# Row maxima turned in 32x32 blocks on VectorE, and other turns put in pairs at six places of four groups

## What is computed

```python
def ffn(x):                      # on (4, 128) tokens in the reference's set-up, here on each sequence
    x = x + msa(layernorm(x, ln1_w, ln1_b), w_qkv, w_proj)      # 16 heads of 8
    return x + moe(layernorm(x, ln2_w, ln2_b), ...)             # 8 experts, hidden 512, best one by gate

x = x + 0.5 * ffn(_layernorm(x))
x = x + attn(_layernorm(x))      # 16 heads of 8, 4 key/value heads, rotary positions
x = x + 0.5 * ffn(_layernorm(x))
# each attention: scores = q @ k.T * scale; softmax over 512 keys; @ v
```

## Time and profile before

| | |
|---|---|
| median of 3 runs | 1510.23 us |
| lowest, highest | 1509.4, 1512.35 us |
| the profiled execution's own time | 1509.52 us |
| its span, first to last instruction | 1507.8 us |
| mean granted TensorE clock | 0.977 |
| TensorE matmul, VectorE, ScalarE, GpSimd busy | 1377.5, 1176.0, 1102.9, 646.7 us |

### The profile page before, as it was taken

One profiled execution on the slowest core, in us unless ns is written; L12 is line 12 of the kernel. 1 busy time (PEld: TensorE's weight loads), 2 busy tenths in 40 slices (PEclk: granted clock), 3 DMA queues, 4 the chain that ended last, 5 costly groups with the idle time before them and its releaser, 6 DMA issues.

```text
span 1507.8 us, 34954 instructions
## 1 busy us (share of the span) xinstructions
PE 1377.5 (91%) x12036; PEld 670.6 (44%) x12036; DVE 1176.0 (78%) x1898; ACT 1102.9 (73%) x2124; POOL 646.7 (43%) x983
## 2 busy tenths in 40 slices
PE   3899999999999997999999999999999999999995
PEld 1333333433338883333333333333333344335995
DVE  6888889888855348888888888888888888894541
ACT  2488877787785563888888888787878777777553
POOL 5224245542226683544364353323334543313753
PEclk8799999999999997999999999999999999999998
DMA  3644433433102425432333243333333333211234
GB/s 90 164 137 117 111 102 98 114 93 86 45 25 60 119 75 160 114 83 69 97 97 83 71 110 86 100 91 79 89 93 84 81 88 100 63 37 37 75 106 120
DMA packets 101485, 137.57 MB, mean 91 GB/s; under 512 B 29792, under 2 KB 72160, under 8 KB 101312
## 3 DMA queue, kind: packets, MB, share of 16 engines
q1 hardware_dynamic: 70768, 85.69, 19.9%
q0 software_dynamic: 24256, 45.31, 12.3%
q10 hardware_dynamic: 6288, 4.34, 1.0%
HBM read 79.05 MB, written 53.51 MB: 88 GB/s over the span
## 4 chain that ended last, share of the span: by engine, by line
PE 58%; DVE 28%; issue 7%; DMA 3%; POOL 2%; ACT 1%; SPq 0%; DVEq 0%; POOLq 0%; ACTq 0%
DVE maxima L1251 25%; PE banks L884 16%; PE banks L871 12%; PE banks L855 11%; PE banks L1610 4%; PE banks L912 4%; PE banks L1619 4%; PE banks L894 2%; PE banks L938 2%; PE banks L919 1%; DMA by_token<-work 1%; PE banks L954 1%; DVE split L1259 1%; DVE stats L1329 1%; DMA work<-sorted_x 1%
## 5 line engine op out<-in xcount | busy, mean ns | idle before, releaser
L1251 DVE TENSOR_REDUCE maxima<-banks 128x2 f32<-128x1024 f32 x768 | 924.1, 1222 | 154.9 <-PE banks L855 146.8
L1222 ACT ACTIVATE work<-banks 128x512 f32<-128x512 f32 x1536 | 829.6, 598 | 155.5 <-PE banks L871 140.6
L855 PE MATMUL banks<-K,Q 64*128 64x512 f32 x1536 | 568.2, 459 | 46.5 <-DVE maxima L1251 36.4
L871 PE MATMUL banks<-Q,K 64*128 64x512 f32 x1536 | 566.2, 450 | 0.5
L884 PE MATMUL banks<-work,V 128*18 128x256 f32 x6144 | 481.6, 386 | 1.5 <-ACT work L1222 0.8
L855 PEld LDWEIGHTS banks<-K,Q 64*128 64x128 f32 x1536 | 228.2, 189 | 200.8 <-DVE maxima L1251 135.4
L871 PEld LDWEIGHTS banks<-Q,K 64*128 64x128 f32 x1536 | 228.9, 185 | 177.4 <-ACT work L1222 128.3
L884 PEld LDWEIGHTS banks<-work,V 128*18 128x18 f32 x6144 | 103.3, 96 | 275.1 <-issue 199.8
L723 POOL TENSOR_TENSOR lo<-full,hi 128x512 fp32r<-128x512 f32 x40 | 51.1, 1278 | 245.6 <-ACT hi L1097 144.1
L1619 PE MATMUL banks<-w,work 128*128 x736 | 99.6, 279 | 0.6 <-ACT work L1653 0.6
L1673 DVE COPY work<-w 128x512 f32 x88 | 43.9, 499 | 71.8 <-PE banks L1610 58.6
(11 more groups left out here) (193 smaller groups left out, 1268.4 us busy)
## 6 DMA issues: line engine op xcount, KB each, us to landing
Q<-q_scratch SPq DMA_DIRECT2D x188, 128.0 KB, 2.6
K<-k_scratch SPq DMA_DIRECT2D x376, 64.0 KB, 2.5
Q<-zero_rows SPq DMA_DIRECT2D x182, 64.0 KB, 2.2
q_scratch<-hi POOLq DMA_DIRECT2D x40, 256.0 KB, 4.7
q_scratch<-lo POOLq DMA_DIRECT2D x40, 256.0 KB, 6.8
k_scratch<-hi POOLq DMA_DIRECT2D x20, 256.0 KB, 4.5
k_scratch<-lo POOLq DMA_DIRECT2D x20, 256.0 KB, 6.3
work<-sorted_x SPq DMA_DIRECT2D x76, 66.0 KB, 2.0
```

The lines of the kernel that those rows point to most:

```text
L855: fill(nc.tensor.matmul(bank, q4[parts(j), n % SLOTS, j // 2, qt * P:(qt + 1) * P], k4[parts(j), n % SLOTS, j // 2, :], start=True, stop=T ...
L871: nc.tensor.matmul(scp[x % EXPS][:, :], k4[parts(j), n % SLOTS, j // 2, kt * P:(kt + 1) * P], q4[parts(j), n % SLOTS, j // 2, :], start=Tr ...
L1222: nc.scalar.activation(prob[:, kt, j ^ 1, :], scp[x % EXPS][:, :], ACT.Exp, scale=SCALE).then_inc(s.probs, 1)
L1251: nc.vector.tensor_reduce(c.maxima[:, at:at + 9:8], c.banks[:, k * S:(k + 2) * S].rearrange("p (m n) -> p m n", m=2), AX.X, ALU.max).then_ ...
```

## The change

There are two parts. First, the row maxima no longer go through TensorE and PSUM. VectorE turns the split maxima, 128 x 32 in SBUF, in four blocks of 32x32, right behind the split. Each block then holds 32 of the 128 queries, so SP moves a group's rows with eight DMAs of 16 pieces of 128 B in place of two DMAs of 16 pieces of 512 B. The turn `rows` leaves the plan, and with it its share of the ring.

Second, the other turns of a batch are placed anew within four groups. Before, an FFN batch had turns after eight steps: (0, 0) rows, z; (0, 2) out, q; (1, 0) rows, n; (1, 2) gate; (2, 0) rows, k; (2, 2) out, v; (3, 0) rows, a; (3, 2) proj, where the first number is n mod 4. Now there are six: (0, 0) z; (0, 2) out, q; (1, 0) n, k; (1, 2) gate, v; (2, 2) out, a; (3, 0) proj. For an attention batch they are z; out, q; qs, k at (1, 0); ks, v at (2, 0); out, a; proj.

```diff
-CONSUMER = {"max": "dve", "rows": "dve", "out": "dve", "gate": "dve", "z": "act", "q": "act", "qs": "act", "k": "act",
+CONSUMER = {"max": "dve", "out": "dve", "gate": "dve", "z": "act", "q": "act", "qs": "act", "k": "act",
...
+        merged = 0 <= n < self.last
+        if merged and kt == 2 and self.attended(n + 1) is not None and n + 1 < self.last:
+            names += [("a", self.attended(n + 1))]
+        if self.attended(n) is not None and not merged:
             names += [("a" if kt == 0 else "proj", self.attended(n))]
+        elif self.attended(n) is not None and kt == 0:
+            names += [("proj", self.attended(n))]
...
         if r == 1 and self.has((n + 7) // G) and not self.ffn((n + 7) // G):
-            names += [("qs" if kt == 0 else "k", (n + 7) // G)]
-        if r == 2 and self.has((n + 6) // G):
+            names += [("qs", (n + 7) // G)] * (kt == 0) + [("k", (n + 7) // G)] * (kt == 2 * (not merged))
+        if r == 1 and merged and self.has((n + 7) // G) and self.ffn((n + 7) // G):
+            names += [("v" if kt else "k", (n + 7) // G)]
+        if r == 2 and merged and self.has((n + 6) // G) and not self.ffn((n + 6) // G) and kt == 0:
+            names += [("ks", (n + 6) // G), ("v", (n + 6) // G)]
+        if r == 2 and not merged and self.has((n + 6) // G):
...
-        if kt == 0 and 1 <= n + 1 < self.last:
-            names += [("rows", n + 1)]
...
             def rows_of_max(n):
                 g = n % SLOTS
-                if n:
-                    released(sp, "rows", n)
-                else:
-                    sp.wait_ge(s.first, 2)
+                sp.wait_ge(s.max_turned, n + 1)
                 for tile in range(2):
                     r = TILE * tile + ROWS
-                    sp.dma_start(c.Q[r:r + 2, ...].rearrange("i (a n) -> i a n", n=P),
-                                 c.maxT[16 * tile:16 * tile + 16, n % 2 * P:(n % 2 + 1) * P].bitcast(F32))
+                    dst = c.Q[r:r + 2, ...].rearrange("i (a b q) -> i a b q", b=4, q=32)
+                    for b in range(4):
+                        at = 32 * b + 16 * tile
+                        sp.dma_start(dst[:, :, b, :], c.maxT[at:at + 16, 32 * (n % 2):32 * (n % 2) + 32])
...
             def split_max(n):
...
+                if n >= 2:
+                    dve.wait_ge(s.max_rows[(n - 2) % SLOTS], 128 * ((n - 2) // SLOTS + 1))
+                dve.wait_ge(s.split, n + 1)
+                nc.vector.transpose(cols(c.maxT, 32 * (n % 2), 32), cols(c.split, 32 * (n % 2), 32).bitcast(F32))\
+                    .then_inc(s.max_turned, 1)
-            def turn_max(n):
...
-            def copy_rows(n):
...
-        c.maxT = sb("maxT", [32, 2 * P], F32R)
+        c.maxT = sb("maxT", [P, 2 * 32])
```

More of the change, by code:

```diff
@@ L359, in slot @@
             names += [("rank", self.ranked(n))]
-        if self.attended(n) is not None:
+        merged = 0 <= n < self.last
+        if merged and kt == 2 and self.attended(n + 1) is not None and n + 1 < self.last:
+            names += [("a", self.attended(n + 1))]
+        if self.attended(n) is not None and not merged:
             names += [("a" if kt == 0 else "proj", self.attended(n))]
+        elif self.attended(n) is not None and kt == 0:
+            names += [("proj", self.attended(n))]
         if self.renormed(n) is not None:
@@ L396, in stream @@
     if True:
-        s = sems(ctx, nc, f"s{label}", "filled freed evacuated first max_hi split recip max_rows:5 q_loaded:5 k_loaded:5 "
+        s = sems(ctx, nc, f"s{label}", "filled freed evacuated max_hi split max_turned recip max_rows:5 q_loaded:5 k_loaded:5 "
                  "scores probs pv out_copied links dve_links first_stored:2 var_ready std_ready normed renormed stats:2 moments:2 added combined roped hi lo:2 "
@@ L594, in rows_of_max @@
                 g = n % SLOTS
-                if n:
-                    released(sp, "rows", n)
-                else:
-                    sp.wait_ge(s.first, 2)
+                sp.wait_ge(s.max_turned, n + 1)
                 for tile in range(2):
                     r = TILE * tile + ROWS
-                    sp.dma_start(c.Q[r:r + 2, g * KSLOT:(g + 1) * KSLOT].bitcast(F32).rearrange("i (a n) -> i a n", n=P),
-                                 c.maxT[16 * tile:16 * tile + 16, n % 2 * P:(n % 2 + 1) * P].bitcast(F32))\
-                        .then_inc(s.max_rows[g], 16)
+                    dst = c.Q[r:r + 2, g * KSLOT:(g + 1) * KSLOT].bitcast(F32).rearrange("i (a b q) -> i a b q", b=4, q=32)
+                    for b in range(4):
+                        at = 32 * b + 16 * tile
+                        sp.dma_start(dst[:, :, b, :], c.maxT[at:at + 16, 32 * (n % 2):32 * (n % 2) + 32])                            .then_inc(s.max_rows[g], 16)
             def opening():
@@ L654, in main @@
                 for g in range(SLOTS):
-                    sp.wait_ge(s.max_rows[g], 32 * len(range(g, last, SLOTS)))
+                    sp.wait_ge(s.max_rows[g], 128 * len(range(g, last, SLOTS)))
                 if label == 0:
@@ L975, in group @@
                 for kind, i in plan.groups.get((n, kt), ()):
-                    if kind == "rows":
-                        turn_max(i)
-                    elif kind == "rank":
+                    if kind == "rank":
                         rank(i)
@@ L1011, in step @@
                 if kt == 0:
-                    pe.wait_ge(s.max_rows[n % SLOTS], 32 * (n // SLOTS + 1))
+                    pe.wait_ge(s.max_rows[n % SLOTS], 128 * (n // SLOTS + 1))
                     if m < last:
@@ L1048, in main @@
                     pe.wait_ge(blocks.s.out_copied, HALVES * NBLK)
-                turn_max(0)
                 loaded(1)
@@ L1309, in group @@
                 for kind, i in plan.groups.get((n, kt), ()):
-                    if kind == "rows":
-                        copy_rows(i)
-                    elif kind == "out":
+                    if kind == "out":
                         normalise(i)
@@ L1502, in main @@
                 split_max(0)
-                copy_rows(0)
                 all_maxima(1)
```

## The result

The changed kernel takes 1522.23 us (median of four runs, 1520.73 to 1525.52), the kernel before, beside it on the same chip, 1511.29 (1509.4 to 1513.11). The ratio is 1.0075, interval 1.0054 to 1.0097: slower by 11 us, where I had put 2.8 us by medians (1513.0 against the 1510.23 known then) and 3.5 by the sum. The profiled executions are 16.0 us apart (1525.52 against 1509.52), and so are the spans.

What follows compares the result with a forecast made beforehand. It took TensorE and VectorE both to be full in a plain step. Terms -21.5 (places), +23.0 (block turns) and +2.0 (starts) sum to +3.5 on the profiled 1509.52: 1513.0 us, range 1505 to 1521, widened to 1500 to 1526.

Steps and rivals of the forecast that it cites:

- The places: Steps followed by other turns of the ring, where VectorE idles for the next fill; placing the turns anew: -21.5 us.
- The method: Pricing a step's extra turns: 0.80 us, hiding TensorE work up to 1.1, or else all of that TensorE work.
- plain step: A step without other turns behind it: 2.44 to 2.46 us, with both TensorE and VectorE full.
- Rival 1: Packed turns hide their work as single ones do, at a flat 0.80: -33.6, total 1501 us; chance 0.22.
- The block turns: On VectorE between split and next reduction: 0.21 for the operation, 0.25 in all, exposed at 92 of 96: +23.0 us.
- Rival 2: The block turn between split and next reduction is dear: 0.39 each, +13 over the sum, 1526 us; chance 0.13.
- The starts: First steps of both streams: -1.1 each, but +3.0 waiting for group 0's rows at the second; +2.0 taken.
- SP in the steady state: Six more row issues of 0.69, 4.1 us a group, are covered by SP's idle 6.6 a group.
- sign of being wrong: One of three named: TensorE waiting for the rows' DMA in mid-stream.
- Rival 3: SP becomes the bound from 1.0 us an issue; at 1.05, +38, total 1550 us; chance 0.04.
- Rival 4: ScalarE, 73% busy, takes over as the pace; half of gain and half of price vanish: 1512 us; chance 0.06.

Runs made afterwards that it cites:

- turn_twice: stores_wait plus a second block turn of the same tile behind the first, into a tile nobody reads; ratio 1.0064 to the kernel before.
- turn_late: stores_wait with only the block turn moved, from behind the split to behind the second reduction of step (n + 1, 0); ratio 0.9958, 1505 us.
- stores_wait: The changed kernel with GpSimd's early stores of Q and K waiting until group 0's eight row DMAs have landed; ratio 0.9998, 1511 us.
- add_mid: stores_wait with GpSimd's addition of the projection put between its normalising and its counting at (3, *); ratio 0.9944, 1503 us.
- place_only: The changed kernel's new placement without the block turn: rows turned by TensorE, two row DMAs as in the kernel before; ratio 1.0047, 1518 us.
- q_store_later: split_late with GpSimd's store of Q put behind its rotation of K in attention batches; ratio 0.9723, 1493.9 us.
- split_late: stores_wait with the whole split and the block turn moved behind the second reduction of step (n + 1, 0); ratio 0.9855, 1489 us.

## Why the prediction was right in direction and short in size

1. **The places** (-21.5 predicted). The steps of both streams together grew by 6.4. Taking off 28.8 for the 90 turns in them and 7.2 for stretches leaves -29.6. By kind of batch that is about -9.8 in full FFN batches (-5.0 predicted), -9.5 in those without a gate turn (-6.8), -2.9 in attention batches (-4.3; some 3 us of late rows are in it) and -7.5 in the last ones (-5.4). The method held: (1, 2) 4.87 for 4.85, attention (1, 0) and (2, 0) 4.00 and 3.96 for 4.18 and 4.14, (3, 2) 2.39 for 2.44. Mis-sized were (1, 0), 3.54 for 3.77, where the two turns hold TensorE for 1.45 (277.92 to 279.37) and not 1.58, and start 1.25 behind the step's first reduction and not 1.36 as in the earlier trace rows; and (2, 0) and (2, 1), 2.37 for 2.56. Behind the latter stands my premise that a plain step of 2.44 leaves VectorE no room. Only TensorE is full there: a reduction can start 1.13 behind the start of the one before, so VectorE catches up where TensorE lets it. Rival 1, a flat price, is out as a mechanism, since (1, 2) rose by its work; that its -33.6 is nearer to the measured sum than my -21.5 does not rest on its mechanism.
2. **The block turns** (+23.0). The operation is 0.21, as taken. The 0.32 measured, 29.4 in all 92, was within my bounds; mis-sized were the gap behind the operation it needs (0.11, I had 0.04 from between the split's two) and the overlap with the next. turn_twice and turn_late show together that it is the dependence that costs. Rival 2 named the right place; its price of 0.39 was too high.
3. **The starts** (+2.0). This step failed. I wrote that the first stream has fewer loads ahead of its rows and only gains 1.1, and that in the second the rows land 2.2 after the last issue. The trace has +7.2 there and +6.7 in the stretch with the second start, and stores_wait gave back 12 us. I had counted SP's own queue, and not that POOL's stores follow within 3 us of the first issue, while eight issues take 5.3; the two DMAs of before were issued ahead of them (from 44.29 in 1.35, the stores from 46.61). The exemption of moves inside SBUF that I had cited from the Trainium skill (DMA: Bandwidth & Descriptors, Why small descriptors are slow (HBM only)) was no protection, though not because of the pieces' size: in stores_wait they land 1.7 behind the last issue.
4. **A cost not on the list:** stretched splits, 7.2 us more than before. I followed the moved projection to its place on TensorE, but not to GpSimd's addition and from there to VectorE. add_mid shows its worth, place_only that it comes from the placement.
5. **SP in the steady state** was covered in the main, as I said, but not wholly. Outside the starts TensorE waits for the rows seven times, 5.5 us in all and all in the second stream; I had named such a wait as a sign of being wrong. Rival 3 is out: 738 of the 768 issues take 0.61 to 0.65, and the 16 of 1.7 or more are too few to stop all groups. Rival 4 is out too: steps without a place are down to 2.24 to 2.39, so their gain did come out, and ScalarE is as busy as before.

By the traces, the 16.0 are my 3.5, 11.9 more at the starts (13.9 for 2.0), 6.4 more for the turns, 7.2 for stretches, 8.1 less for places, and 4.9 less for what stands behind the last reduction, of which I had forecast nothing and no run shows the cause. So costs of 25 us that I had missed were set off in part by 13 us of gains that I had missed too: that the time lies inside my range is luck as far as the starts and the stretches go. Why the medians differ by 11 only stays open; the profiled execution of the change was the slowest of its four, that of the kernel before (1509.52) lies near its fastest, and the late rows are a wait that need not be the same each time.

## What to carry to other kernels

When a transfer is cut into more and smaller ones, look for the next large transfer on any queue, not only for room on its own. An operation put between others costs the distance to the result that it needs, so put a chain of small ones where the engine waits anyway: that, and keeping stores from the rows, made this change worth 2.8% instead of costing 0.75%. When work moves, follow it to its last consumer, and see what runs beside that one.

## What was unexpected of the hardware

- A VectorE operation of 0.17 on SBUF that starts during GpSimd's two-input operation of 128x512 ends with it and takes 1.03 in the change, up to 1.27 in q_store_later; seen on copies, on a two-input maximum and, in split_late (1.14), on the second operation of the split.
- Eight SBUF-to-SBUF DMAs of 2 KB in pieces of 128 B landed within 2 us of the last issue when alone, and some 9 us later with six 256 KB stores issued by POOL beside them. In the changed kernel, 44 to 60 us, the share of each queue was this:

```profile
q0 software_dynamic: 864, 1.58, 48.5%
q1 hardware_dynamic: 2008, 1.05, 22.2%
```

- The same stretch slowed the X loads' issues on SP, five in 10.3 us for 2.6.
- VectorE: an operation that needs the result of one of 0.17 starts 0.21 (the split's second) to 0.28 (the block turn) behind its start; an independent one 0.09 to 0.14. Reductions of 128x1024 from PSUM start 1.13 apart when nothing holds them, though one lasts 1.22.
